# A fused attention-and-non-local kernel: VectorE's order in image 0, the seams between images and the end reordered

## The chip, the cores and the metric

The kernel runs on one core of one Trainium2 chip. The metric is the device time of one launch in microseconds (us), the median of several runs. Four images are worked through in one launch; inputs and outputs lie in HBM.

## What is computed

Two layers run one after the other on `x` of shape (4, 32, 32, 256).

```python
# layer 0: deformable attention and an MLP, per image
q      = layernorm(x) @ wq + bq
off    = conv1x1(gelu(depthwise_conv7x7_stride2(q)))       # 2 x 16 x 16 offsets
interp = grid_sample(x, refs + tanh(off))                  # 256 sampled rows
k = v  = interp @ wv + bv
attn   = softmax(heads(q @ mq) @ heads(k @ mk).T)          # 8 heads, 1024 x 256
z      = (attn @ heads(v @ mv)) @ mo + mo_b + x
y      = gelu(layernorm(z) @ mlp + mlp_b) + z
# layer 1: non-local block, per image
attn1  = softmax(theta(y) @ maxpool(phi(y)).T)             # 1024 x 256
out    = y + sigma * ((attn1 @ maxpool(g(y))) @ w_o + b_o)
```

## The kernel before, in words

Every engine has its own program, written out by hand as a list of steps; semaphores tie them together. Nothing is scheduled by a planner: an engine does its steps strictly in the order of its list, and a step that waits holds back all that stands behind it on that engine.

**Slots.** An image's attention is cut into eight units (`unit_at`: half of the rows, group of four heads, quarter of the rows). The main loop has one slot per unit, `(b, s)` with `b` the image and `s` from 0 to 7 (`slots`), and runs one slot list beyond the last image in a function `tail`. In slot `s` a unit's work is spread over three slots, so four units are in flight:

- unit `s`: `scores` in two halves (TensorE, L834, into the only score bank `ps_s`), each followed by `maxima` (VectorE, L1672), which drains that bank;
- unit `s - 1`: `max_rows` (TensorE transposes the maxima, L842), `max_out` (ScalarE, L1270), `maxima_lo` (VectorE, L1677), then two small DMAs from GpSimd's queue (`max_row`, L1982) that lay the maxima beside the queries;
- unit `s - 2`: `shifted` in two parts (TensorE, L853, into the only bank `ps_t`), each followed by `exps` (ScalarE, L1278), which drains it into `prob`;
- unit `s - 3`: `values_mixed` (TensorE, prob times values, L870) and `values_summed` (TensorE, prob times ones, L876), both into the only bank `ps_v`; then `denominators` (ScalarE, L1287 and L1289: the reciprocal as Ln and Exp) and `normalise` (VectorE, L1686), which drains `ps_v`.

`joined(b, s)` says how the two value steps lie in a slot. With None, `values_mixed` stands before the second half of the scores and `values_summed` after it, behind the second `shifted` part. With "first" both stand side by side before the second half of the scores, ScalarE makes the denominators between its two `exps`, and VectorE normalises before the second `maxima` (in slot 5 after it). With "last" both stand behind the second `shifted` part.

**Work of the neighbours.** Between these steps each slot carries dense work: the front of the next image `n` (row statistics `row_stats`, `row_scale`, `row_shift` on VectorE; `q_image`, `conv`, `offsets`, `queries`, `keys` on TensorE; `positions`, the `gather` by GpSimd's indirect DMA, `corner_weights` and `sampled`) and the back of the previous ones (`project`, `turn_rows`, `mlp_rows`, `turn_output`, `project1`, `scores1`, `max_rows1`, `shifted1`, and for the image before that `sums1`, `mix1`, `result_rows`). All dense products share a ring of three PSUM banks, in the order that `dense_order` writes out; a product waits until the one three places ahead of it has been drained.

**Image 0.** VectorE's slot 2 of image 0 has `row_stats` for image 2 (eight statistics, which wait for the loads of `xa`), ahead of the second `maxima`, and `row_scale` (eight tiles) at its end. Slots 5 and 6 have the eight steps of `sampled` for image 1, which combine the gathered corners; `corner_weights` stands in slot 4, `positions` and the gather in slot 3. In slot 6 `bias_rows` stands at the end, in slot 7 `row_shift` (half of the tiles of image 2) and `fold`.

**Seams.** In slot 7 of images 1 and 2 the non-local block of the image before takes its last maxima: `max_rows1` (L958), `max_out1` (ScalarE, L1331), `maxima1_lo` (VectorE, L1762), two small DMAs `max_row1` (GpSimd's queue, L2021), then `shifted1` (L966). SyncE's queue carries the six `stack_k` transfers of the next image at the same time. In slot 0 of image 2 VectorE has `residual_norm`, `row_shift` (the other half of the tiles, L1558), then `result` (L1786 to L1791 and L1777), which drains the banks of `mix1` (L997).

**The end.** `tail(m)` finishes image 3 and the results of image 2: `turn_rows` (L897), `norm_turned` (ScalarE, L1294), `mlp_rows` (L920), `mix1` (L997), `turn_output` (L931).

## Time and profile before

| what | value |
|---|---|
| median of 3 runs | 481.4 us (479.86 to 481.94) |
| the profiled execution's own time | 484.76 us |
| its span, first to last instruction | 482.9 us |
| mean granted TensorE clock over the span | 0.988 of full |
| TensorE busy with matmuls | 445.8 us, 92% of the span |
| VectorE, ScalarE, GpSimd busy | 60%, 43%, 23% of the span |

Times in the trace are microseconds from the start of the span. PE is TensorE's matmul stream, PEld its weight loads, DVE VectorE, ACT ScalarE, POOL GpSimd, SP SyncE. A wait is idle time of an engine just before an instruction, put down to the engine or transfer that ended last. The profiled execution lies 3.4 us above the median of the runs.

### The profile page before, as it was taken

What the parts mean: (1) busy time and instruction counts of PE and PEld (TensorE: products, weight loads), DVE (VectorE), ACT (ScalarE), POOL (GpSimd) and SP (SyncE); (2) the same over time, 40 slices, a digit from 0 to 9 for tenths busy, and PEclk for the clock granted to TensorE, in tenths of its full rate; (3) what the DMA queues carried; (4) which work ended last, traced back from release to release, by engine and by line L of the source; (5) the groups of instructions that cost most, each with busy time, mean ns of one, the idle gap of its engine ahead of it and who ended that gap; (6) DMA issues with size and microseconds to landing.
All of it is one profiled execution on the core that took longest, in us unless ns stands there. A gap on an engine that the chain in (4) does not pass through costs nothing.

```text
span 482.9 us, 9296 instructions
## 1 busy us (share of the span) xinstructions
PE 445.8 (92%) x3733; PEld 315.8 (65%) x3733; DVE 288.0 (60%) x617; ACT 209.9 (43%) x338; POOL 110.8 (23%) x150
## 2 busy tenths in 40 slices
PE   7899898797999999998999999999999998988976
PEld 6767665555668676756678666756767674655755
DVE  3719644858784277768763365476647747726343
ACT  1122113455346145765426245854273584672350
POOL 5510501041002000692002002781021030100000
PEclk9999999889999999999999999999999998999999
DMA  7498858574857960394029910494137110000112
GB/s 213 104 176 110 155 92 173 94 155 117 105 112 102 182 147 3 90 126 74 2 104 123 191 15 3 114 107 67 45 77 102 47 43 2 1 3 0 48 41 88
DMA packets 30488, 42.90 MB, mean 89 GB/s; under 512 B 6075, under 2 KB 21230, under 8 KB 30446
## 3 DMA queue, kind: packets, MB, share of 16 engines
q1 hardware_dynamic: 23742, 34.95, 39.7%
q0 software_dynamic: 3584, 4.50, 3.7%
q10 hardware_dynamic: 3120, 2.86, 3.0%
q8 instruction: 30, 0.49, 0.5%
q14 instruction: 12, 0.10, 0.1%
HBM read 16.16 MB, written 4.19 MB: 42 GB/s over the span
## 4 chain that ended last, share of the span: by engine, by line
PE 56%; DVE 16%; DMA 10%; ACT 6%; issue 5%; POOL 3%; ACTq 2%; SPq 1%; DVEq 0%; POOLq 0%
PE ps_d L785 7%; PE ps_d L920 6%; PE ps_d L887 5%; PE ps_d L997 5%; PE ps_v L870 5%; PE ps_s L834 4%; PE ps_v L876 4%; PE ps_t L853 4%; DMA xa<-in_x_dram 3%; PE ps_d L773 3%; PE ps_d L939 3%; DVE mx L1672 3%; PE ps_d L805 3%; ACTq L430 2%; DMA q_st<-mx_t 2%
## 5 line engine op out<-in xcount | busy, mean ns | idle before, releaser
L1278 ACT ACTIVATE prob<-ps_t 128x1024 f32<-128x1024 f32 x64 | 65.4, 1022 | 81.3 <-PE ps_t L853 80.2
L1672 DVE TENSOR_REDUCE mx<-ps_s 128x4 f32<-128x1024 f32 x64 | 78.2, 1222 | 19.5 <-PE ps_s L834 18.2
L1982 POOL DMA_DIRECT2D q_st<-mx_t x64 | 33.9, 531 | 235.7 <-ACT mx_t L1270 216.7
L785 PE MATMUL ps_d<-cstack,conv_w 128*32 128x256 f32 x1024 | 58.3, 380 | 0.2 <-DMA cstack<-att 0.2
L834 PE MATMUL ps_s<-k_st,q_st 96*128 96x256 f32 x256 | 49.5, 316 | 6.3 <-DVE mx L1672 4.5
L785 PEld LDWEIGHTS ps_d<-cstack,conv_w 128*32 128x32 f32 x1024 | 35.3, 108 | 21.0 <-issue 2.0
L834 PEld LDWEIGHTS ps_s<-k_st,q_st 96*128 96x128 f32 x256 | 36.3, 192 | 17.9 <-DVE mx L1672 10.9
L853 PE MATMUL ps_t<-q_st,k_st 98*128 98x256 f32 x256 | 42.8, 290 | 2.6 <-ACT zt L1336 1.0
L853 PEld LDWEIGHTS ps_t<-q_st,k_st 98*128 98x128 f32 x256 | 35.7, 193 | 5.0 <-issue 2.8
L870 PE MATMUL ps_v<-prob,vh 128*32 128x256 f32 x512 | 35.8, 398 | 2.1 <-DVE att L1686 2.1
L876 PE MATMUL ps_v<-prob,ones 128*32 128x256 f32 x512 | 35.2, 393 | 0.0
L887 PE MATMUL ps_d<-mo,att 128*128 128x256 f32 x128 | 29.7, 379 | 0.3 <-DVE att L1686 0.3
L1686 DVE TENSOR_TENSOR att<-ps_v,rden 128x256 f32<-128x256 f32 x32 | 13.4, 420 | 25.5 <-ACT rden L1289 23.0
L887 PEld LDWEIGHTS ps_d<-mo,att 128*128 128x128 f32 x128 | 23.7, 190 | 3.5 <-issue 0.5
L1677 DVE TENSOR_TENSOR mx_t<-ps_d,mx_t 4x256 fp32r<-4x256 f32 x32 | 13.3, 414 | 18.5 <-ACT mx_t L1270 17.9
L773 PE MATMUL ps_d<-wq,xln 128*128 128x256 f32 x96 | 22.4, 383 | 2.0 <-DVE xln L1558 1.7
L876 PEld LDWEIGHTS ps_v<-prob,ones 128*32 128x32 f32 x512 | 16.3, 113 | 11.3 <-issue 1.6
L2033 POOL DMA_INDIRECT corners<-in_x_dram,row_of x16 | 16.0, 999 | 33.2 <-DVE row_of L1613 29.6
L997 PE MATMUL ps_d<-gwo,zt 128*128 128x256 f32 x96 | 22.4, 384 | 0.2
L1777 DVE SCALAR_TENSOR_TENSOR z_all<-ps_d,rd,z_all 128x256 f32<-128x256 f32 x32 | 13.9, 479 | 14.3 <-PE ps_d L997 14.2
L870 PEld LDWEIGHTS ps_v<-prob,vh 128*32 128x32 f32 x512 | 14.1, 111 | 12.6 <-issue 4.4
L1270 ACT ACTIVATE mx_t<-ps_d 4x256 fp32r<-4x256 f32 x32 | 11.6, 362 | 24.6 <-PE ps_d L842 24.6
(180 smaller groups left out, 741.0 us busy)
## 6 DMA issues: line engine op xcount, KB each, us to landing
q_st<-q_parts SPq DMA_DIRECT2D x42, 256.0 KB, 5.6
xa<-in_x_dram SPq DMA_DIRECT2D x8, 512.0 KB, 8.4
z_all<-in_x_dram SPq DMA_DIRECT2D x8, 512.0 KB, 7.8
out_dram<-z_all SPq DMA_DIRECT2D x8, 512.0 KB, 2.6
cstack<-qpad SPq DMA_DIRECT2D x22, 180.5 KB, 5.7
k_st<-cstack SPq DMA_DIRECT2D x23, 128.0 KB, 3.4
q_st<-z_all SPq DMA_DIRECT2D x6, 256.0 KB, 7.0
cstack<-att SPq DMA_DIRECT2D x6, 180.5 KB, 5.3
```

The lines of the kernel that those rows point to most:

```text
L773: ins = pe.matmul(ps[:, jj, :], xln_tile(b)[:, t, cb * P:(cb + 1) * P], wq[:, kt, :], start=kt == 0, stop=kt == 1)
L785: ins = pe.matmul(ps[32 * k:32 * k + 32, 0, :], conv_w[:, cb * 4 + k, y, x, :], cstack[:, cb, k, y:y + HG_, x:x + WG_], start=n == 0, stop ...
L834: ins = pe.matmul(ps_s[:, h, :], q_st[0:96, hg * HQ + h, c0 + half * P:c0 + (half + 1) * P], k_st[0:96, b % 2, h, hg, :], start=True, stop ...
L853: ins = pe.matmul(ps_t[:, 2 * hh + mt, :], k_st[0:98, b % 2, h, hg, mt * P:(mt + 1) * P], q_st[0:98, hg * HQ + h, c0:c0 + S_], start=True, ...
L870: pe.matmul(ps_v[32 * h:32 * h + 32, 0, :], vh[:, mt, hh * HD:(hh + 1) * HD], prob[:, u % 2, h, mt, :], start=mt == 0, stop=mt == 1)
L876: ins = pe.matmul(ps_v[32 * h:32 * h + 32, 1, :], ones[:], prob[:, u % 2, h, mt, :], start=mt == 0, stop=mt == 1)
L887: ins = pe.matmul(ps[:, jj, :], att[:, hg, cb * HALF + j * P:cb * HALF + (j + 1) * P], mo[:, hg, :], start=hg == 0, stop=hg == 1)
L920: ins = pe.matmul(ps[:, jj, :], turned_tile(b)[:, kt, cb * HALF + j * P:cb * HALF + (j + 1) * P], mlp[:, kt, :], start=kt == 0, stop=kt == 1)
L997: ins = pe.matmul(ps[:, jj, :], turned_tile(b)[:, mt, cb * HALF + j * P:cb * HALF + (j + 1) * P], gwo[:, mt, :], start=mt == 0, stop=mt == 1)
L1278: drain(act.activation(prob[:, u % 2, 2 * pr:2 * pr + 2].rearrange("p h m s -> p (h m) s"), ps_t[:], ACT.Exp), t_ring, "t", b, u, pr)
L1672: drain(dve.tensor_reduce(mx[:, u % 2, half, :], ps_s[:], AX.X, ALU.max), s_ring, "s", b, u, half)
L1982: pool.dma_start(q_st[96 + part:97 + part, hg * HQ:(hg + 1) * HQ, c0:c0 + S_].bitcast(F32), mx_t[32 * part:32 * part + HQ, u % 2, :].bitca ...
```

## The change

It reorders steps and changes no arithmetic.

- Image 0: `joined` gives "first" in slots 4 to 6. On VectorE `row_stats` moves behind the second `maxima` of slot 2; `row_scale` is split, four tiles in slot 3 and four in slot 7, both behind the second `maxima`; the first half of `sampled` moves from slot 5 to the end of slot 4.
- Slot 7 of images 1 and 2: `joined` gives "last" instead of "first"; the first `project` product moves ahead of the second half of the scores.
- Slot 0 of image 2: a new value "ahead" puts both value steps and `sums1` before the first `shifted` part; VectorE's `row_shift` moves behind `result`.
- The end: the second product of `mix1(m - 1, 0)` moves ahead of `mlp_rows(m, 1)`, and its `result_rows` ahead of `outputs(m, 1, [0])`.

```diff
 def joined(b, s):
     if not b or b == B:
-        return None
-    if s == 3 or s == 6 and b < B - 1:
+        return "first" if not b and 4 <= s <= 6 else None
+    if s == 3 or s in (6, 7) and b < B - 1:
         return "last"
-    return "first" if s in (2, 4, 5, 7) or s == 1 and b < B - 1 or s == 0 and 2 <= b < B - 1 else None
+    if s == 0 and 2 <= b < B - 1:
+        return "ahead"
+    return "first" if s in (2, 4, 5, 7) or s == 1 and b < B - 1 else None
...
@@ dense_order @@
-    order += [("mlp", m, 1, jp) for jp in range(2)] + [("o", mm, 0, 1), ("o", mm, 1, 0)]
+    order += [("o", mm, 0, 1)] + [("mlp", m, 1, jp) for jp in range(2)] + [("o", mm, 1, 0)]
...
@@ TensorE, slot @@
                 if (s, b) != (0, 1):
                     scores(b, s, 0)
+                if joined(b, s) == "ahead":
+                    values(*unit_of(b, s, 3))
+                    sums1(mm)
                 if unit_of(b, s, 2):
                     shifted(*unit_of(b, s, 2), 0)
...
                 if s == 0 and fin:
-                    sums1(mm)
+                    if b >= B - 1:
+                        sums1(mm)
                     mix1(mm, 0)
...
+                if s == 7 and 0 < b < B - 1:
+                    project(b, 0, 0)
...
                     for lh in range(2):
-                        project(b, 0, lh)
+                        if lh or b == B - 1:
+                            project(b, 0, lh)
                         if post:
                             shifted1(m, lh)
...
@@ TensorE, tail @@
                 turn_rows(m, 1)
+                mix1(m - 1, 0, [1])
                 mlp_rows(m, 1)
-                mix1(m - 1, 0, [1])
...
@@ VectorE, slot @@
-                if in_front(b, s, "qimg0") and b:
+                if in_front(b, s, "qimg0") and 0 < b < 2:
                     row_shift(n, range(NJ, NT))
-                if s == 2 and b == 0:
-                    row_stats(n + 1)
...
                 if s == 0 and fin:
                     result(mm)
+                if in_front(b, s, "qimg0") and fin:
+                    row_shift(n, range(NJ, NT))
...
-                if joined(b, s) == "first" and s != 5:
+                early = joined(b, s) in ("ahead", "first") and s != 5
+                if early:
                     normalise(*unit_of(b, s, 3))
                 if cur:
                     maxima(b, s, 1)
-                if b == 0 and s in (5, 6):
-                    sampled(n, s - 5)
-                if unit_of(b, s, 3) and (joined(b, s) != "first" or s == 5) and (s, b) != (6, B - 1):
+                if (b, s) == (0, 6):
+                    sampled(n, 1)
+                if s == 2 and b == 0:
+                    row_stats(n + 1)
+                if s in (3, 7) and b == 0:
+                    row_scale(n + 1, range(NJ) if s == 3 else range(NJ, NT))
+                if unit_of(b, s, 3) and not early and (s, b) != (6, B - 1):
                     normalise(*unit_of(b, s, 3))
+                if (b, s) == (0, 4):
+                    sampled(n, 0)
...
-                if s == 2 and b == 0:
-                    row_scale(n + 1, range(NT))
...
@@ VectorE, tail @@
                 result_rows(m - 1, 0, [0])
+                result_rows(m - 1, 0, [1])
                 outputs(m, 1, [0])
-                result_rows(m - 1, 0, [1])
```

ScalarE's `denominators` and TensorE's conditions on `joined` follow the new value "ahead" as they do "first".

## Rows read from the trace of the kernel before

**Rows 1.** The page: busy time of each engine, and TensorE's clock in 40 slices

```profile
PE 445.8 (92%) x3733; PEld 315.8 (65%) x3733; DVE 288.0 (60%) x617; ACT 209.9 (43%) x338; POOL 110.8 (23%) x150
PEclk9999999889999999999999999999999998999999
```

**Rows 2.** Waits of TensorE, whole span: us in total, times, longest us

```profile
PE ps_s L834 <- DVE mx L1672: 4.5, 6, 1.2
PE ps_d L842 <- DVE mx L1672: 3.0, 4, 2.1
...
PE ps_t L966 <- DMA th_st<-mx_t: 2.4, 2, 1.4
PE ps_v L870 <- DVE att L1686: 2.1, 3, 0.8
...
PE ps_t L853 <- ACT zt L1336: 1.0, 2, 0.5
```

**Rows 3.** Timeline, image 0, slots 2 and 3: start, us, instructions, [idle before <- releaser]

```profile
86.92 1.41 DVE L1529 BATCH_NORM_STATS2 st<-xa 128x6 f32<-128x256 f32 x4 [0.39 <-DMA xa<-in_x_dram]
...
88.92 1.19 DVE L1672 TENSOR_REDUCE mx<-ps_s 128x4 f32<-128x1024 f32 x1
90.02 3.25 DVE L1547 SCALAR_TENSOR_TENSOR xa<-xa,mv,lng_all 128x256 f32<-128x256 f32 x8
...
90.25 0.38 PE L842 MATMUL ps_d<-consts,mx 128*4 128x128 f32 x2 [2.10 <-DVE mx L1672]
...
92.42 0.17 ACT L1241 ACTIVATE pos<-ps_d 128x4 f32<-128x4 f32 x1 [1.37 <-PE ps_d L797]
...
93.90 1.02 ACT L1278 ACTIVATE prob<-ps_t 128x1024 f32<-128x1024 f32 x1
...
95.03 1.23 PE L834 MATMUL ps_s<-k_st,q_st 96*128 96x256 f32 x4 [0.99 <-DVE mx L1672]
```

**Rows 4.** Windows: stretch, length, busy PE, PEld, DVE, ACT, POOL, clock, DMA share, GB/s

```profile
92.50:99.40 6.90, 5.91 (x43) 3.19 (x36) 4.61 (x12) 3.78 (x5) 2.52 (x3) 0.51 0.44 73
...
107.77:113.49 5.72, 4.49 (x52) 2.96 (x51) 3.86 (x6) 2.87 (x4) 1.04 (x2) 1.00 0.52 185
113.49:119.40 5.91, 4.55 (x54) 3.03 (x51) 4.91 (x9) 3.11 (x6) 1.04 (x2) 1.00 0.07 25
```

**Rows 5.** Timeline, image 0, slots 4 to 6, and image 1, slot 1 (146 us)

```profile
103.23 1.07 PE L876 MATMUL ps_v<-prob,ones 128*32 128x256 f32 x16
...
105.23 0.42 DVE L1686 TENSOR_TENSOR att<-ps_v,rden 128x256 f32<-128x256 f32 x1 [1.09 <-ACT rden L1289]
...
111.34 0.74 PE L834 MATMUL ps_s<-k_st,q_st 96*128 96x256 f32 x4 [1.23 <-DVE mx L1672]
...
113.64 1.53 DVE L1649 SCALAR_TENSOR_TENSOR samp<-corners,corner_w,samp 128x256 f32<-128x256 f32 x3
...
115.64 1.07 PE L870 MATMUL ps_v<-prob,vh 128*32 128x256 f32 x16 [0.82 <-DVE att L1686]
...
146.10 1.07 PE L870 MATMUL ps_v<-prob,vh 128*32 128x256 f32 x16
...
146.97 1.07 PE L876 MATMUL ps_v<-prob,ones 128*32 128x256 f32 x16
```

**Rows 6.** DMA issues with us to landing: 60:135, then 218:232, then 400:420

```profile
corners<-in_x_dram,row_of POOLq DMA_INDIRECT x4, 6.3
...
th_st<-mx_t POOLq DMA_DIRECT2D x2, 4.0 KB, 3.2
...
th_st<-mx_t POOLq DMA_DIRECT2D x2, 4.0 KB, 1.6
```

**Rows 7.** Image 2, slot 0: VectorE's timeline, and a wait of TensorE (216 to 250 us)

```profile
238.22 1.66 DVE L1558 SCALAR_TENSOR_TENSOR xln<-xa,rs,lnb_all 128x256 f32<-128x256 f32 x4
...
PE ps_d L897 <- DVE z_all L1777: 0.7, 1, 0.7
```

**Rows 8.** Waits of TensorE at the end, 440 to 460 us

```profile
PE ps_d L920 <- ACT xln L1294: 1.0, 1, 1.0
```

More of the change, by code:

```diff
@@ L1018, in slot @@
                     offsets(n)
-                if unit_of(b, s, 3) and joined(b, s) != "last" and (s, b) != (6, B - 1):
+                if unit_of(b, s, 3) and joined(b, s) not in ("ahead", "last") and (s, b) != (6, B - 1):
                     values_mixed(*unit_of(b, s, 3))
@@ L1074, in slot @@
                     values_mixed(*unit_of(b, s, 3))
-                if unit_of(b, s, 3) and joined(b, s) != "first" and (s, b) != (6, B - 1):
+                if unit_of(b, s, 3) and joined(b, s) not in ("ahead", "first") and (s, b) != (6, B - 1):
                     values_summed(*unit_of(b, s, 3))
@@ L1351, in slot @@
                     exps(*unit_of(b, s, 2), 0)
-                if joined(b, s) == "first":
+                if joined(b, s) in ("ahead", "first"):
                     denominators(*unit_of(b, s, 3))
@@ L1368, in slot @@
                     exps(*unit_of(b, s, 2), 1)
-                if unit_of(b, s, 3) and joined(b, s) != "first":
+                if unit_of(b, s, 3) and joined(b, s) not in ("ahead", "first"):
                     denominators(*unit_of(b, s, 3))
```

## The prediction, made before the changed kernel ran

> **What bounds the kernel now.** I read the page first. TensorE is busy 92% of the span and VectorE 60% [rows 1], so TensorE's stream sets the time. Only two things can shorten it: its waits, and stretches in which its clock is low. The work itself hardly changes. TensorE's waits by releaser come next [rows 2]: 4.5 us in six waits of the second half of the scores for `maxima`, 3.0 us in four waits of the transposed maxima, 2.1 us of `values_mixed` for `normalise`, 2.4 us in two waits for the small DMAs of the non-local maxima, and two waits of 0.5 us of `shifted` for the non-local exponentials. The change touches nearly all of them.
>
> The timeline then says why. In slot 2 of image 0 VectorE stands in `row_stats`, waiting for `xa` to land (86.92), so the second `maxima` comes only at 88.92 and TensorE idles 2.10 us until 90.25. Then eight tiles of `row_scale` (3.25 us) hold back the next `maxima`: 0.99 us more at 95.03 [rows 3]. Right behind these idle times the granted clock is 0.51 for 6.9 us, in which TensorE is busy 5.91 us [rows 4]; that is the lower of its two levels, 1.2 GHz against 2.4. In slots 5 and 6 TensorE works 4.49 and 4.55 us of 5.72 and 5.91 [rows 4]; there VectorE's list is too long, four sampling steps (1.53 us for three of them) in each [rows 5].
>
> **The change, part by part.**
>
> *Image 0, slots 2 to 4.* The second `maxima` no longer waits behind `row_stats`: -2.10. Four tiles of `row_scale` instead of eight, and behind the second `maxima`: -0.99 [rows 3]. `row_stats` still waits for the same landing; queued behind it is now only the next slot's `maxima_lo`, whose input comes at about the same time (88.9). In slot 4 the sums stand before the second scores and cover its 0.54 us wait, one of the six of [rows 2]. Work done at half clock takes double, so if the slow stretch does not come 5.91/2 = 2.9 us go; I take 2.7, since a part of the 5.91 lies in its edges. Against this: the second `shifted` part of slot 3 must wait for the first `exps`. That starts 1.48 us after the tanh (table load between: 92.42 to 93.90) and takes 1.02 [rows 3], so it ends 2.5 us after `offsets`, while TensorE at full clock has only the mixed values (1.07) and scores to do, about 1.6. New wait: 0.95. The values of slot 4 then wait 0.2 for `normalise`, since from the end of the sums to the end of `normalise` it is 105.65 - 104.30 = 1.35 us [rows 5]. Side by side the two value steps start 0.87 apart (146.10 and 146.97) [rows 5] instead of 1.0: -0.13. Sum: -2.10 - 0.99 - 0.54 - 2.7 + 0.95 + 0.2 - 0.13 = **-5.3**.
>
> Here a rule speaks about the clock term. The Trainium skill (TensorE: Matmul & The Clock Gate, What's actually happening) says that the throttled state is the default, that activity releases it, and that the hardware's window runs freely, so that the transition point varies from run to run. The trace agrees in that 2.10 us of idleness precede the fall; the idle times of 1.0 to 1.5 us elsewhere mostly have none behind them. By that rule the 2.7 could be absent from some runs before, and a fall could come in some runs after; both are among the rivals.
>
> *Image 0, slots 5 and 6.* They hold 9.04 us of work and 2.59 us of waits [rows 4]. The waits shown (1.23 and 0.82 [rows 5], and another 0.54) go, and merging gives -0.26. But `values_summed` used to cover the second `maxima`: now nothing stands between the second `shifted` part and the next slot's transposes, which need that `maxima`. In slot 5 `maxima` starts when the scores end, takes 1.2 us, and TensorE has only `shifted` (0.6) to do: 0.85 with the semaphores and what its delay hands on. In slot 6 `normalise` stands ahead of it and itself waits 0.93 us (105.23 - 104.30 [rows 5]) for the sums: 1.5. Slot 5's second scores wait 0.28 for `maxima`, which now stands behind `query_lo`. 2.63 of new waits: **-0.3** for both slots. Most of what is taken out of these two slots comes back as another wait.
>
> The first half of `sampled` (1.9 us) now needs its corners some 10 us earlier. Median landing is 6.3 us after issue [rows 6]; the gather starts about 4.7 us earlier than before, so I put the landing at the very moment at which slot 4 reaches it. Queued behind are `query_lo`, slot 5's `maxima`, and with them the scores. If the corners are late each us counts; bound 0 to +2, I take 0, since the same gather ran beside query stacking in the trace too.
>
> *Image 0, slot 7.* The 0.82 us wait of the values for `normalise` that remained goes (L870 waits three times in all) [rows 2], since VectorE's `sampled` no longer stands before it; `bias_rows` (1.3 us) then lies in front of the next `maxima` and costs 0.1. Four tiles of `row_scale` (1.6 us, half of 3.25 [rows 3]) fill the time in which ScalarE makes the denominators. **-0.7**.
>
> *Slot 7 of images 1 and 2.* No values stand ahead of the non-local maxima's transposes, so the small DMAs start 1.3 us earlier, and the values cover their flight. Waits now: 1.35 and 1.06 [rows 2]. With key stacking in flight they land 3.2 us (median) after issue, without it 1.6 [rows 6]. Two readings: the latency stays near 3, then 0.95 and 1.06 are gained; or the landing is tied to the end of key stacking, then 0.35 and 0.5. I take the middle: **-0.65 and -0.8**. Ends: 0 and -2.4 for the pair.
>
> A rule of the Trainium skill (DMA: Bandwidth & Descriptors, Queues, rings and completion order) bears on this: each DMA engine takes turns between its queues packet by packet. By it the earlier issue would not stand behind the key transfers, and the pair would give -2.0 rather than my -1.45.
>
> *Slot 0 of image 2.* The values and sums before the first `shifted` part cover its 0.51 us wait (L853) [rows 2]. `row_shift` (1.66 us) leaves the path to `result_rows`, which frees the bank that `turn_rows` waits 0.7 us for [rows 7]; with 0.1 beside it, -0.74. `row_shift` itself is needed by `q_image` only, 5 us later. **-1.25**. ScalarE's denominators come later, but nobody needs them soon.
>
> *The end.* `mix1` (half: 1.9 us of work that has to be done anyway) fills the 1.0 us in which `mlp_rows` waits for ScalarE [rows 8]. The bank is free and `outputs` still comes in time: **-1.0**.
>
> Sum: -5.3 - 0.3 - 0.7 - 1.45 - 1.25 - 1.0 = **-10.0 us**. The profiled execution took 484.8 us (span 482.9), so it would take about 474.8. The timed runs have a median of 481.4, 3.4 us less, and some of that may be a slow stretch that they lack. I keep the whole sum: 471.4 us.
>
> **The rivals.**
>
> *Clock.* The gain of the clock does not come, either because timed runs did not have the stretch at 92 us, or because new waits (0.95 in slot 3, 1.5 in slot 6) bring one. For: the page shows one other fall, at 398 to 411 us, after much smaller idle times, and the median is 3.4 below the profiled run. Against: 2.10 us is by far the longest idle time in the loop. Time: 481.4 - 7.3 = 474.1, with a new fall of 1.5 us 475.6. Chance 0.22.
>
> *Transfers.* The corners, and the maxima of unit 3 that GpSimd issues right behind them, come late because the gather now overlaps with query stacking; slot 5 waits up to 3 us, and the gain of slot 7 of images 1 and 2 does not come (+1.45). 481.4 - 5.5 = 475.9. For: all share 16 DMA engines. Against: 1.6 us is enough when they are free. Chance 0.12.
>
> *More gain.* The second slow stretch of the page also goes, by another phase or shift, worth about 1.6 us: 469.8. Chance 0.08.
>
> *No change.* The DVE chain of image 0 is the true bound and the next transfers take back everything, or the timed runs differ little from one another: 480.5. Against it stand the seams and the end, whose 3.7 us do not hang on image 0. Chance 0.04.
>
> *Slower.* Place: slots 3 to 7 of image 0. If the 0.95 and 1.5 us waits keep TensorE at the low level from 92 to 119 us, its 22 us of work there take 44. Some 6 us of the extra lie in waits, 2.9 were paid before: +13 against a rest of -7.3, 487. It decides where the granted clock is 0.5 for more than 14 us of image 0. For it: the fall at 92 us lasted through slot 3. Against: with waits of 1.23, 0.82 and 0.82 the clock was 1.00 in slots 5 and 6 [rows 4]. Chance 0.03.
>
> **How the numbers follow.** The forecast with its sizes as above has 0.51. Its own spread is about 3 us either way. A measurement of this kernel can tell about 0.5%, 2.4 us, from no change. Faster by more: 0.51 + 0.22 + 0.12 + 0.08 = 0.93, less 0.02 for the tail of the transfer case: 0.91. Within: 0.06. Slower: 0.03. The range goes from 468.0, where the small DMAs give their full 2.4 and the second slow stretch goes, to 477.5, where neither clock nor transfers help.
>
> **What would show it.** TensorE's 2.10 and 0.99 us waits gone, clock 1.00 from 88 to 100 us; new waits of the transposes (L842) for `maxima` at the ends of slots 5 and 6, near 0.85 and 1.5; slot 7 of image 0 reached about 5.5 us earlier and image 1 about 6.3; L966 waiting under 1 us in all; no waits of L897 for `result_rows` in image 2 or of L920 at the end. It is wrong if the clock stays low in slot 3 or 4, if `sampled` in slot 4 waits for corners, or if image 1 starts less than 4 us earlier.

## The result, and the profile after

Six runs of the changed kernel have a median of 475.94 us (475.23 to 478.65); six of the kernel before beside them 481.67. The ratio is 0.990 (95% interval 0.986 to 0.994). The time was forecast at 471.4, in a range of 468.0 to 477.5. The measured time lies inside the range, but the gain is 5.7 us by the medians and 4.9 by the ratio, about half of the 10.0 us of the sum. The profiled execution took 478.56 us, its span is 476.7.

The page: TensorE's work is the same [rows 1].

```profile
PE 444.0 (93%) x3733; PEld 316.6 (66%) x3733; DVE 288.3 (60%) x617; ACT 209.8 (44%) x338; POOL 111.2 (23%) x150
...
PEclk9999999998899999999999999999999999999999
```

The low clock at 92 us is gone, and another has come further on, in the tenth and eleventh slices. The second fall of the kernel before, in slice 34 (398 to 411 us), is absent here too; more on both below. TensorE's waits over the whole span (us in total, times, longest), beside [rows 2]; from line 130 on, line numbers are 2 to 14 higher than in the kernel before:

```profile
PE ps_d L844 <- DVE mx L1681: 3.4, 5, 1.5
...
PE ps_t L855 <- DMA q_st<-mx_t: 1.9, 3, 1.0
PE ps_s L836 <- DVE mx L1681: 1.7, 3, 0.7
...
PE ps_t L968 <- DMA th_st<-mx_t: 1.5, 2, 1.1
...
PE ps_v L872 <- issue: 0.6, 1, 0.6
```

The scores' waits for `maxima` (L836) fell from 4.5 us to 1.7. The transposes (L844) wait longer, 3.4 for 3.0, and `shifted` (L855) waits 1.9 us for small DMAs instead of 0.7. One of its three waits, 0.7 us before 86 us, is in both kernels; the two new ones, 1.14 us together, are for the DMAs of units 3 and 4 of image 0. Waits of L899 for `result_rows` and of L922 at the end no longer appear [rows 7, 8].

Where they stand, on the timeline of image 0, slots 3 (from 87.5 us) to 6 (to 117.9), against [rows 3, 5]:

```profile
92.25 0.73 PE L855 MATMUL ps_t<-q_st,k_st 98*128 98x256 f32 x4 [0.93 <-ACT prob L1287]
...
95.84 1.07 PE L872 MATMUL ps_v<-prob,vh 128*32 128x256 f32 x16 [0.59 <-issue]
...
98.29 0.65 PE L878 MATMUL ps_v<-prob,ones 128*32 128x256 f32 x4 [0.35 <-issue]
...
104.47 0.74 PE L855 MATMUL ps_t<-q_st,k_st 98*128 98x256 f32 x4 [0.17 <-DMA q_st<-mx_t]
...
109.15 0.38 PE L844 MATMUL ps_d<-consts,mx 128*4 128x128 f32 x2 [0.93 <-DVE mx L1681]
...
110.97 0.74 PE L855 MATMUL ps_t<-q_st,k_st 98*128 98x256 f32 x4 [0.97 <-DMA q_st<-mx_t]
...
117.87 0.38 PE L844 MATMUL ps_d<-consts,mx 128*4 128x128 f32 x2 [1.50 <-DVE mx L1681]
```

The three waits that the prediction gave 0.95, 0.85 and 1.5 us are there with 0.93, 0.93 and 1.50. Four others were not in the sum, or larger than in it. The wait of 0.59 has no releaser in the profile, but the program says what it is: `values_mixed` may not write `ps_v` before `normalise` has drained it. In ScalarE's and VectorE's timelines `denominators` start 0.36 us late and `normalise` ends at 95.69, 0.15 us before the values start:

```profile
94.41 0.38 ACT L1296 ACTIVATE rden<-ps_v 128x256 f32<-128x256 f32 x1 [0.36 <-PE ps_v L878]
...
95.27 0.42 DVE L1695 TENSOR_TENSOR att<-ps_v,rden 128x256 f32<-128x256 f32 x1 [1.00 <-ACT rden L1298]
```

The windows of slots 3 to 6 of image 0, each from transposes to transposes, and the two stretches of low clock (columns as in [rows 4]):

```profile
87.53:93.92 6.39, 5.46 (x63) 3.91 (x59) 6.12 (x24) 4.11 (x6) 2.31 (x4) 1.00 0.52 68
93.92:103.44 9.52, 8.58 (x63) 5.00 (x60) 6.44 (x17) 5.02 (x11) 3.80 (x5) 1.00 0.92 194
103.44:109.15 5.71, 4.61 (x51) 3.14 (x50) 4.48 (x7) 3.67 (x6) 1.04 (x2) 1.00 0.53 185
109.15:117.87 8.72, 6.24 (x51) 3.59 (x51) 3.53 (x6) 3.36 (x6) 1.04 (x2) 0.80 0.55 80
111.60:115.00 3.40, 3.40 (x33) 1.39 (x32) 0.11 (x1) 1.02 (x1) 0.00 (x0) 0.50 0.48 93
118.40:121.80 3.40, 3.40 (x24) 1.91 (x23) 3.27 (x7) 1.28 (x2) 0.84 (x2) 0.51 1.07 125
```

From 87.53 to 109.15 the clock is full. The two low stretches hold 6.8 us of work done at 1.2 GHz instead of 2.4, 3.4 us more than at full clock: as much as the one of before [rows 4] cost (2.9 us), and a little over. The first stands 0.6 us behind the wait of 0.97 and 2.5 us behind that of 0.93; the second 0.5 us behind that of 1.50. Where the falls stand differs from one profile of this same kernel to the next. In its second profile (e13) the first stands in slot 3, right behind the wait of `shifted` for `exps` that the change itself brought (0.93 us, ending at 92.6), so the low clock at 92 us is not gone for good:

```profile
92.70:96.10 3.40, 3.40 (x23) 1.82 (x24) 1.82 (x5) 1.41 (x2) 2.79 (x3) 0.50 0.51 124
116.60:120.00 3.40, 3.40 (x26) 2.16 (x24) 3.27 (x7) 1.40 (x2) 0.54 (x2) 0.50 1.08 125
```

The seams, TensorE's waits in slot 7 of image 1 and slot 0 of image 2 (212 to 250 us), then in the same stretch an image later (316 to 350):

```profile
PE ps_t L968 <- DMA th_st<-mx_t: 1.1, 1, 1.1
...
PE ps_t L968 <- DMA th_st<-mx_t: 0.4, 1, 0.4
```

On the timeline from one slot's transposes to the next, slot 7 of image 1 is 0.2 us shorter than before, slot 0 of image 2 1.6, slot 7 of image 2 0.7 and the end 1.2: 3.7 in all, forecast 3.7. So the whole shortfall lies in image 0 and in the clock.

The two profiled executions differ by 6.2 us of span (482.9 and 476.7), and image 0 has almost none of it. Its slot 3 begins 2.7 us earlier (87.53 for 90.25), slot 7 begins 1.5 us earlier, and image 1 begins (transposes of its slot 0) at 134.34 for 135.24, 0.9 us earlier, of which 0.57 were there at 72 us already, before the first step that the change moves. The prediction had called itself wrong if image 1 started less than 4 us earlier. Another 1.6 us come from the stretch between the transposes at 404 and 417 us, on which the change does not bear: there the kernel before ran 3.4 us at 1.2 GHz, and the changed kernel did not. That fall comes and goes in these kernels (the pages of six of the sixteen experiments show it), so the 1.6 us are not the change's. The window of the kernel before:

```profile
406.60:410.00 3.40, 3.40 (x32) 1.80 (x35) 2.48 (x4) 1.02 (x1) 0.52 (x1) 0.50 0.03 7
```

and of the changed kernel:

```profile
403.00:410.00 7.00, 7.00 (x63) 5.31 (x62) 5.73 (x9) 3.22 (x5) 1.56 (x3) 1.00 0.02 5
```

### The profile page after: what moved, and what is told of

Same layout as the page of the kernel before. It is cut to its first block, busy times and chain, and to the rows that moved or that the text cites. A ratio compares the mean times of both kernels' runs of the same rounds, so it can differ in the third digit from the quotient of the medians.

```text
span 476.7 us, 9296 instructions
## 1 busy us (share of the span) xinstructions
PE 444.0 (93%) x3733; PEld 316.6 (66%) x3733; DVE 288.3 (60%) x617; ACT 209.8 (44%) x338; POOL 111.2 (23%) x150
## 4 chain that ended last, share of the span: by engine, by line
PE 57%; DVE 16%; DMA 11%; ACT 6%; issue 5%; POOL 3%; SPq 1%; ACTq 0%; DVEq 0%; POOLq 0%
PE ps_d L787 9%; PE ps_d L922 6%; PE ps_d L889 5%; PE ps_d L999 5%; PE ps_v L872 5%; PE ps_t L855 4%; PE ps_s L836 4%; PE ps_v L878 4%; PE ps_d L775 3%; PE ps_d L941 3%; DMA xa<-in_x_dram 3%; DMA q_st<-mx_t 3%; PE ps_d L807 3%; DVE mx L1681 2%; DMA th_st<-mx_t 2%
## 5 line engine op out<-in xcount | busy, mean ns | idle before, releaser
L836 PE MATMUL ps_s<-k_st,q_st 96*128 96x256 f32 x256 | 49.0, 314 | 3.0 <-DVE mx L1681 1.7
L787 PEld LDWEIGHTS ps_d<-cstack,conv_w 128*32 128x32 f32 x1024 | 36.3, 108 | 19.9 <-issue 2.0
L855 PE MATMUL ps_t<-q_st,k_st 98*128 98x256 f32 x256 | 42.9, 290 | 4.2 <-DMA q_st<-mx_t 1.9
L836 PEld LDWEIGHTS ps_s<-k_st,q_st 96*128 96x128 f32 x256 | 35.8, 189 | 14.2 <-DVE mx L1681 7.2
L855 PEld LDWEIGHTS ps_t<-q_st,k_st 98*128 98x128 f32 x256 | 35.5, 192 | 7.4 <-DMA q_st<-mx_t 2.8
L807 PE MATMUL ps_d<-xln,w_qh 128*128 128x512 f32 x48 | 22.2, 594 | 0.0
L1279 ACT ACTIVATE mx_t<-ps_d 4x256 fp32r<-4x256 f32 x32 | 11.6, 363 | 23.9 <-PE ps_d L844 23.9
L922 PE MATMUL ps_d<-mlp,zt 128*128 128x256 f32 x96 | 22.0, 382 | 0.0
```

The source lines that it names most:

```text
L787: ins = pe.matmul(ps[32 * k:32 * k + 32, 0, :], conv_w[:, cb * 4 + k, y, x, :], cstack[:, cb, k, y:y + HG_, x:x + WG_], start=n == 0, stop ...
L807: ins = pe.matmul(ps[:].rearrange("p a s -> p (a s)"), w_qh[:, kt, hg * P:(hg + 1) * P], xln_tile(b)[:, kt:NT:2, half * P:(half + 1) * P], ...
L836: ins = pe.matmul(ps_s[:, h, :], q_st[0:96, hg * HQ + h, c0 + half * P:c0 + (half + 1) * P], k_st[0:96, b % 2, h, hg, :], start=True, stop ...
L855: ins = pe.matmul(ps_t[:, 2 * hh + mt, :], k_st[0:98, b % 2, h, hg, mt * P:(mt + 1) * P], q_st[0:98, hg * HQ + h, c0:c0 + S_], start=True, ...
L922: ins = pe.matmul(ps[:, jj, :], turned_tile(b)[:, kt, cb * HALF + j * P:cb * HALF + (j + 1) * P], mlp[:, kt, :], start=kt == 0, stop=kt == 1)
```

## How the runs are compared

The mean granted clock differs from run to run of one kernel, and the time with it: the 68 runs of the kernel before that stand beside the experiments give 338 us of time per unit of clock lost, all kernels of this study, each about its own mean, 337 (without the two longest of the 68 runs 325 and 331; no difference below depends on which is taken). I therefore give two numbers for each kernel: the median and ratio as measured, and **the time at full clock**, which is the mean time less 338 us times the mean clock lost. Before: 482.13 us at a mean clock of 0.9909, so 479.05 at full clock (standard error 0.1). The changed kernel, 12 runs, six of them under e13: 476.18 at 0.9942, so 474.2 (error 0.4). The change gained 4.8 us in waits and 1.1 in clock, with an error of about 0.4 on each. "At full clock" is an estimate; where it and the ratios as measured disagree, I say so.

## The experiments

```
kernel                      median  ratio to before (95%)    mean clock  at full clock
e1  image 0 only            479.40  0.995 (0.991 to 0.998)   0.9931      477.5
e2  seams and end only      476.98  0.988 (0.984 to 0.992)   0.9933      474.7
e3  image 0 apart           474.70  0.984 (0.980 to 0.988)   0.9950      473.4
e4  later z load            475.80  0.987 (0.983 to 0.991)   0.9915      472.9
e5  waits filled            475.41  0.985 (0.980 to 0.989)   0.9942      473.2
e6  statistics only         479.15  0.996 (0.993 to 1.000)   0.9942      477.8
e7  apart, gather split     474.49  0.985 (0.981 to 0.989)   0.9950      473.1
e8  gather split            475.90  0.987 (0.982 to 0.991)   0.9917      472.6
e9  sampled back            477.76  0.992 (0.989 to 0.995)   0.9912      474.8
e10 mixed                   475.92  0.988 (0.984 to 0.992)   0.9932      473.2
e11 mixed, query deferred   472.96  0.985 (0.981 to 0.990)   0.9962      472.7
e12 before, wait filled     482.18  1.001 (0.999 to 1.003)   0.9932      479.6
e13 changed kernel again    475.83  0.987 (0.983 to 0.991)   0.9940      473.7
e14 late stacking           476.50  0.989 (0.985 to 0.992)   0.9918      473.5
e15 split and back          474.38  0.985 (0.982 to 0.988)   0.9934      472.6
e16 mixed again             474.37  0.983 (0.980 to 0.986)   0.9960      472.4
```

The times at full clock have standard errors of 0.2 to 0.7. e1, e6, e9 and e12 have 12 runs each, e15 and e16 5, the others 6; each ratio is to runs of the kernel before on the same chip. Where no other base is named, an edit is against the changed kernel.

### e1 and e6: image 0's part alone, and of it only the statistics

e1 is the kernel before with all of image 0's edits (the first bullet of the change) and none of the others. e6 is the kernel before with `row_stats` and `row_scale` alone:

```diff
-                if s == 2 and b == 0:
-                    row_stats(n + 1)
...
                     sampled(n, s - 5)
+                if s == 2 and b == 0:
+                    row_stats(n + 1)
+                if s in (3, 7) and b == 0:
+                    row_scale(n + 1, range(NJ) if s == 3 else range(NJ, NT))
...
-                if s == 2 and b == 0:
-                    row_scale(n + 1, range(NT))
```

> The kernel before with only the image 0 parts of the change (side by side in slots 4 to 6, VectorE's new order). Theory: image 0 gives back what it wins, through new waits of the transposes for maxima at the ends of slots 5 and 6 (0.9 and 1.5 us), a wait of shifted for its small DMA in slot 6 (1.0 us) and granted-clock falls behind them: 0 to 2.5 us faster than before, 479 to 481.5 us. Rival: image 0 wins its 6 us in most runs and the seams fail there: 475.5 us.

> The kernel before with only row_stats and row_scale moved on VectorE in image 0. Theory: the 2.1 and 1.0 us waits of TensorE at the start of slot 3 and in it go, one 0.95 us wait of shifted for exps comes, and the clock fall behind them goes or gets shorter: -2.1 us of waits and -1 to -2.7 of clock, 478 to 479.5 us against 482. Rival, the wait moves on whole (row_stats delays maxima_lo instead): 481 us or more.

e1 gained 1.5 us at full clock where 3.6 were forecast for these parts, and 2.3 in the mean with the clock, where 6.3 were. e6 gained 1.2, and its median of 479.15 is as expected: most of what image 0 gives comes from those two steps, and `joined`, `sampled` and slot 7 add some 0.3, which is less than its error of 0.5. e1's median, 479.40, fits the theory and excludes its rival (475.5). TensorE's waits from 86 to 134 us, first e1:

```profile
PE ps_d L842 <- DVE mx L1672: 2.4, 2, 1.5
PE ps_t L853 <- DMA q_st<-mx_t: 1.6, 1, 1.6
PE ps_v L870 <- issue: 1.0, 1, 1.0
PE ps_t L853 <- ACT prob L1278: 0.9, 1, 0.9
```

and e6:

```profile
PE ps_v L870 <- DVE att L1686: 1.5, 3, 0.8
PE ps_t L853 <- DMA q_st<-mx_t: 1.4, 2, 1.3
```

In both the same wait for the small DMAs has come up, which neither `joined` nor `sampled` can have made, since e6 has neither: it is enough that slots 2 and 3 are shorter. The profiled execution of e1 was at full clock throughout image 0 in spite of waits of 1.6, 1.0 and 1.5 us, so these waits do not bring a fall every time. Its 1.0 us wait of the values is again one for `normalise`, which ends 0.15 us before them; here `denominators` started 0.81 us late.

### e2: the seams and the end alone

The changed kernel with image 0 as before (the first line of the diff, and all of VectorE's edits for `b == 0`, undone).

> The change without its image 0 parts: seams of images 1, 2 and the end only. Theory: these save what the two profiles show, 1.8 (slot 7 of image 1 and slot 0 of image 2) + 0.7 (slot 7 of image 2) + 1.2 (end) = 3.7 us: 477.9 us. Image 0 keeps its 2.1 us wait and the slow stretch. Rival (image 0 carries the gain): within 1.5 us of before, 480 us or more.

The median is 476.98 for the expected 477.9: 4.4 us at full clock, forecast 3.7, its error 0.4. These parts are right, and the rival, that image 0 carries the gain, is excluded. They are also nearly the whole of the changed kernel's 4.8: on top of them image 0 gives 0.5 (error 0.6), not 3.6.

### e3, e7 and e8: value steps apart again, and the gather in two parts

```diff
@@ e3 and e7 @@
-        return "first" if not b and 4 <= s <= 6 else None
+        return None
@@ e7 and e8: the second half of the gather a slot later @@
-                    gather(n)
+                    gather(n, range(1) if b == 0 else range(2))
+                if (b, s) == (0, 4):
+                    gather(n, range(1, 2))
```

With the gather cut, only two of its four DMAs stand in GpSimd's queue ahead of unit 3's small DMAs; those are issued at 96.28 us in e8, where the changed kernel has 97.23, and two gather DMAs fewer are in flight with them. They land 6.3 us after issue in e8 and 5.1 in e7, so part of what the cut gives is the earlier issue.

> The changed kernel with the value steps of image 0 apart again, as before; VectorE's new order stays. Theory: the sums again cover maxima at the ends of slots 5 and 6, the waits of 0.9 and 1.5 us go, no clock fall follows: 2 to 4 us faster than the changed kernel, 472 to 474 us. Rival: values_mixed waits 0.8 us for normalise in each slot as in the kernel before and takes it back: 475.5 to 476.5 us.

> The changed kernel with the value steps of image 0 apart and the gather cut in two. Theory: the two repairs are independent, but with the steps apart slot 5 is bound by VectorE's list, not by the small DMAs: 474 to 474.7 us, no slower than with the steps apart alone (474.7). Rival, the effects add: 473.5 us or less.

> The changed kernel with image 0's gather cut in two: its first half in slot 3, its second behind the small DMAs of unit 3. Theory, transfers: these DMAs no longer stand in GpSimd's queue behind four gathers, the wait of shifted in slot 5 (0.2, 1.1 and 1.7 us in three profiles) and any wait of sampled for corners go: slot 5 near 5.5 us, 0.5 to 1.5 us less than the changed kernel, 474.5 to 475.5 us. Rival, the query stacking alone makes them late: the same waits and time.

None of the three medians settles its expectation cleanly: e3 has 474.70, between theory (472 to 474) and rival (475.5 to 476.5), e7 474.49 inside its theory, e8 475.90 just above its (474.5 to 475.5). Apart, with or without the cut, the kernel is faster by 0.8 to 1.1 us at full clock; the medians of the 12 runs of e3 and e7 together and of the 12 of the changed kernel are 474.5 and 475.9. Resampling these runs gives a ratio of the means of 0.9975 (0.995 to 1.000), from several chips, so this is at the limit of what can be told. So with the gather whole, side by side did not help. With the gather cut (e8 and e7) the two ways are 472.6 and 473.1 at full clock, not to be told apart. The lengths of the slots, each from transposes to transposes, say what side by side does where no transfer is late and no fall lies in the slot:

```
us                  slot 3  slot 4  slot 5  slot 6  slot 7   from
side by side          6.39    7.93    5.71    5.82   14.95   e4; slot 5 of e14
apart                 6.39    8.86    5.71    5.33   15.84   e6; slots 5 to 7 of e7
```

It gains 0.9 in slot 4, nothing in slot 5, loses 0.5 in slot 6, and gives 0.9 in slot 7, since no value wait is left there. The waits of the transposes eat what slots 5 and 6 gain, as forecast; what side by side costs beside that is the cover of the small DMAs, and clock. The 47 runs with it in slots 5 and 6 and these waits left open (changed kernel, e4, e8, e9, e14, e15) have a mean clock of 0.9924 (error 0.0005), the 29 with the steps apart there (e3, e7, e10, e11, e16) 0.9950 (0.0007): 0.9 us. e7's waits, 86 to 134 us:

```profile
PE ps_s L836 <- DVE mx L1681: 2.3, 3, 1.2
PE ps_v L872 <- DVE att L1695: 1.1, 2, 0.8
```

No wait for DMAs is left (nor has e3 one, with the gather whole, in a profile in which a fall made slot 3 1.3 us longer). In e8 none is left either, but VectorE then stood waiting for the corners, and the scores behind it for 1.2 us. VectorE's timeline of e8 in slots 4 and 5:

```profile
102.26 0.35 DVE L1655 TENSOR_SCALAR samp<-corners,corner_w 128x256 f32<-128x256 f32 x1 [1.51 <-DMA corners<-in_x_dram,row_of]
...
104.09 1.41 DVE L1595 SCALAR_TENSOR_TENSOR q_parts<-ps_d,cols,q_parts 128x512 fp32r<-128x512 f32 x2
...
105.97 1.22 DVE L1681 TENSOR_REDUCE mx<-ps_s 128x4 f32<-128x1024 f32 x1
```

`query_lo`, slot 5's lower maxima and its `maxima` queue behind the late corners, as the transfer rival has it. At full clock e8 is still 1.6 us under the changed kernel (error 0.7); its median is the same, since its runs had a lower clock (0.9917).

### e4 and e14: which transfer makes the small DMAs late

```diff
@@ e4, SyncE: the z load a slot later @@
                     if s == 3:
                         behind_max_row(b, 3)
+                    if s == 4:
+                        behind_max_row(b, 4)
                         load_z(b)
@@ e14, SyncE: a query stacking a slot later @@
-                    if s == 2:
-                        behind_max_row(b, 2)
-                        stack_q(b, 1, [1])
                     if s == 3:
                         behind_max_row(b, 3)
+                        stack_q(b, 1, [1])
                         load_z(b)
```

> The changed kernel with image 0's z load issued one unit later, behind the small DMAs of unit 4. Theory: the 1.0 us wait of shifted in slot 6 for these DMAs (behind 1 MB of z load) never occurs; with it one of the two idle times that stood before the first clock fall is gone: 0.5 to 1.5 us less than the changed kernel, 474.5 to 475.5 us. Rival, the wait is seldom there in the timed runs: same within 0.5 us.

> The changed kernel with the stacking of image 0's second query half (one part of it) issued a slot later, behind unit 3's step and ahead of the z load. Theory A, the stacking takes the DMA engines from the gather and the small DMAs: the wait of the first shifted part of unit 3 (1.1 to 1.9 us in most profiles) falls under 0.3, and the corners are there when sampled comes. Theory B, the small DMAs are late because GpSimd's queue has the gather ahead of them: the wait stays at 1.1 to 1.9 us. In either case the first scores that read the half moved may wait, up to 1 us, in slot 6; the median then stays within 0.3% of the changed kernel's.

In e4 (median 475.80, expected 474.5 to 475.5) the wait in slot 6 (110.97 above) is absent, and that in slot 5 is 2.8 us: the z load has no part in the lateness of unit 3's DMAs. That it makes unit 4's late fits, but is not shown: e5, e8, e9 and e15 leave it where it was, and do not have the wait either. For unit 3's DMAs e14 decides. The DMA issues of 95 to 100 us, with us to landing, in e4:

```profile
q_st<-mx_t POOLq DMA_DIRECT2D x2, 4.0 KB, 7.4
```

The same of 94 to 99 us in the changed kernel:

```profile
q0 software_dynamic: 158, 0.52, 50.5%
q1 hardware_dynamic: 256, 0.49, 48.1%
...
q_st<-mx_t POOLq DMA_DIRECT2D x2, 4.0 KB, 6.4
```

and in e14:

```profile
q0 software_dynamic: 287, 0.95, 65.7%
...
q_st<-mx_t POOLq DMA_DIRECT2D x2, 4.0 KB, 2.8
```

q1 is query stacking, q0 the gather with the small DMAs. Together they fill the 16 engines (98.6% in the changed kernel), and 4 KB take 6.4 us to land. In e14 the same four gather DMAs stand ahead of the small ones in GpSimd's queue, stacking is out of the way, and they land in 2.8. The wait of `shifted` for them is gone, and VectorE does not wait for the corners either (0.9 us in e13). So it is query stacking on the shared engines, as theory A has it, not the order of GpSimd's queue. The median did not fall (476.50): the scores of slot 6 now wait 0.7 us for the queries moved and 0.4 more for `maxima`, a fall of the clock begins there (108.5 us), and the mean clock was lower (0.9918). e14's waits, 86 to 134 us:

```profile
PE ps_d L842 <- DVE mx L1679: 2.1, 2, 1.1
...
PE ps_s L834 <- DMA q_st<-z_all: 0.7, 1, 0.7
...
PE ps_s L834 <- DVE mx L1679: 0.4, 1, 0.4
```

### e9 and e15: the first half of `sampled` back in slot 5

```diff
@@ e9 and e15 @@
-                if (b, s) == (0, 6):
-                    sampled(n, 1)
+                if b == 0 and s in (5, 6):
+                    sampled(n, s - 5)
...
-                if (b, s) == (0, 4):
-                    sampled(n, 0)
@@ e15 alone: the gather cut as in e7 @@
```

> The changed kernel with the first half of sampled back in slot 5, steps still side by side. Theory: sampled never waits for its corners (1.5 us in two profiles), but slots 5 and 6 are bound by VectorE's list again and every maxima comes later: 0 to 1.5 us slower than the changed kernel, 476 to 477.5. Rival, the wait for corners is what slot 5 pays: 1 us faster, 475 us or less.

> The changed kernel with the gather cut in two (second half a slot later) and the first half of sampled back in slot 5. No work is left out. Theory of the transfers: no wait of shifted for unit 3's small DMAs and none of sampled for corners; what is left are the waits for maxima, and because VectorE has four sampling steps more in slot 5, slots 5 and 6 together lose 1 to 2 us to maxima. The median is then between the changed kernel's and 0.5% above. Rival, that the DMA waits cost the whole of what is missing: 0.4 to 0.6% below the changed kernel.

e9 takes the early need of the corners away and keeps everything else. Its median of 477.76 is at the upper end of its theory (476 to 477.5) and excludes the rival. It came out at 474.8 at full clock, no better than the changed kernel (474.2): the small DMAs alone cost it 1.9 us in its profile. e15 has neither DMA wait and reaches 472.6; its median of 474.38 lies below its theory (no faster than the changed kernel) and just short of the rival's 0.4 to 0.6% below it. e9 and e15 differ in nothing but the cut, and this is the clearest figure for the lateness of the small DMAs: 2.2 us at full clock (error 0.4), or 1.7 (0.5) if each is taken against the kernel before on its own chip. That corners needed early are worth having once the small DMAs are in time is not shown: e8, which has them early, is at 472.6 as well.

### e5 and e12: do small waits bring the low clock?

Products whose results nobody reads, put on TensorE ahead of the transposes; no wait is taken away.

```diff
@@ e5, changed kernel; e12, kernel before: 4 products if (b, u) == (0, 2) @@
                 ps = open_bank(dense, "mxt", b, u)
+                for _ in range({5: 2, 6: 3}.get(u, 0) if b == 0 else 0):
+                    pe.matmul(ps[:, 1, :], ident, w_kh[:, 0, :], start=True, stop=True)
```

> The changed kernel with two and three dummy 128x256 products (0.43 us each, into the unused half of the transposes' bank) in the two new waits of TensorE at the ends of slots 5 and 6 of image 0. No work is taken away and the waits themselves stay; if they cause the clock falls, the granted clock stays 1.00 through slots 5 to 7: 1 to 2 us less than the changed kernel in the median (474 to 475 us), and no run near 478.5. Rival, the falls have another cause: same time and the same falls, or 0.2 us more.

> The kernel before with four dummy 128x256 products (1.73 us) inside TensorE's 2.1 us wait at the start of image 0's slot 3. The wait and all other work stay. Theory: if the wait brings the clock fall at 92 us, that fall goes; worth up to 2.7 us where it stood, 1 to 2 us in the median since some runs lack it: 480 to 481 us, mean granted clock up by about 0.004. Rival, the tiny products of offsets cause it as well: no difference.

e12 is the experiment on the clock term, with 480 to 481 us expected. It fills the 2.10 us wait that precedes the fall of [rows 4] and leaves the time as it is: 482.18 against 482.06 (ratio 1.001, 0.999 to 1.003). Its windows behind the next wait, that of the scores for `maxima`, 1.74 us at 92.6 to 94.3:

```profile
92.70:94.80 2.10, 0.51 (x4) 0.51 (x5) 1.97 (x6) 1.39 (x2) 0.50 (x1) 1.00 0.02 4
94.80:98.20 3.40, 3.40 (x25) 1.82 (x25) 1.65 (x5) 1.37 (x2) 1.76 (x2) 0.51 0.70 117
```

The work that the first wait had delayed now waited at the second, and the fall came 2 us later behind that one; in this profile it lasted 3.4 us where the kernel before had 6.9. The runs have a mean clock of 0.9932 (error 0.001) for 0.9909, worth 0.8 us, and 0.5 more at full clock takes that back. So filling that wait alone did not give the 2.7 us; a gain of some tenths in clock cannot be excluded. In e5 the profile is free of a fall in slots 4 to 7 and no run is over 477.0, but the median (475.41) misses the 474 to 475 expected, and the mean clock is the changed kernel's, 0.9942: the profile agrees with the theory that filling helps, the six runs do not show it. At full clock e5 is 1.0 us under the changed kernel (error 0.7) though no wait was taken away; differences of this size from six runs can be chance.

### e10, e11, e13 and e16: a better order

```diff
@@ e10, e11 and e16, beside the gather cut of e7 @@
-        return "first" if not b and 4 <= s <= 6 else None
+        return "first" if not b and s == 4 else None
...
-                if (b, s) == (0, 6):
-                    sampled(n, 1)
...
                 if (b, s) == (0, 4):
                     sampled(n, 0)
+                if (b, s) == (0, 6):
+                    sampled(n, 1)
@@ e11 and e16: the second part of query_lo behind slot 5's first maxima @@
+                if (b, s) == (0, 5):
+                    query_lo(n, 0, [1])
...
-                    query_lo(n, 0)
+                    query_lo(n, 0, range(NHG) if b else [0])
```

> The changed kernel with the steps side by side only in slot 4, apart in slots 5 and 6, normalise ahead of the second half of sampled in slot 6, and the gather cut in two. Theory: slot 4 near 7.9 us as side by side, slot 5 near 5.7, slot 6 near 5.3 and the 0.8 us wait of the values in slot 7 gone: 1.5 us less than with the steps apart everywhere, 473 us. Rival, corners come late and VectorE takes it back: 474.5 us.

> As e10_mixed, and the second query_lo of image 1 stands behind slot 5's first maxima instead of before slot 5's maxima_lo. Theory: the 1.2 us wait of the second scores in slot 5 for maxima shrinks by 0.6: 472.5 us. Rival, that wait has moved elsewhere already: same as e10_mixed.

> The changed kernel once more, unaltered, as the control of the three others. If the ratio measured for it holds, 0.990 (0.986 to 0.994) against the kernel before. Theory of the transfers: its profile has at least one of the two waits in slots 4 and 5 of image 0, of the transposes or of shifted for unit 3's small DMAs (0.2 to 1.9 us) or of sampled for the corners. Rival, that those waits were a matter of one profile: none of them.

> The best version once more (side by side only in slot 4, normalise ahead of sampled in slot 6, the gather cut in two, one part of query_lo later), beside the changed kernel on the same chip. If its gain is real: 0.984 to 0.987 against before, and 0.3 to 0.6% under the changed kernel. If its first measurement was luck of the clock: within 0.2% of it.

Side by side in slot 4 only, `normalise` ahead of `sampled` in slot 6, the gather cut: 473.2 at full clock for e10, whose median (475.92) misses the 473 expected. With `query_lo` in two it is 472.7 and, run again, 472.4; what `query_lo` adds is inside the errors. The 11 runs of e11 and e16 have a median of 473.1; against the 12 of the changed kernel the ratio of the means is 0.9952 (0.992 to 0.998, resampled), some 2.3 us. Beside each other on one chip, e16 and e13: 0.983 (0.980 to 0.986) and 0.987 (0.983 to 0.991) of the kernel before. e16 lies 0.4% under e13 in the mean, as expected of a real gain. This version beats both kernels. At full clock it is level with e8 and e15 (472.6); its lead over them as measured, 473.1 for 475.3, goes with the clock (0.9961 for 0.9925). Its profiled execution (e11) took 472.84 us, at full clock in all 40 slices; its waits, 86 to 134 us:

```profile
PE ps_s L836 <- DVE mx L1681: 1.8, 2, 1.1
PE ps_t L855 <- ACT prob L1287: 0.9, 1, 0.9
PE ps_t L855 <- DMA q_st<-mx_t: 0.6, 1, 0.6
PE ps_v L872 <- DVE att L1695: 0.5, 2, 0.2
```

3.8 us in these four lines, where the four of e1 have 5.9. VectorE still waited 1.4 us for the corners in it, and 1.8 in e16. e13's own profile has 0.47 and 0.62 us of `shifted` waiting for small DMAs and 0.9 of `sampled` for the corners, so those waits of the changed kernel were no matter of one profile.

## Why the prediction was right or wrong

**Slots 2 and 3, the order of VectorE.** Right. The 2.10 and 0.99 us waits are gone and 0.93 has come for 0.95; slot 3 takes 6.39 us from transposes to transposes. In e6 these two edits are 1.2 us at full clock, of the 2.1 that the sum has for them; 1.3 us wait there for the small DMAs. One reading was off without effect: the 0.54 us wait of slot 4's second scores is not one of the six for `maxima`, the profile gives it no releaser.

**Slots 5 and 6.** The new waits of the transposes are right to 0.1 us (0.93 for 0.85, 1.50 for 1.5), and so is the reading that side by side gives back what it takes. The terms shown add up to -0.2, not -0.3.

**Image 0 as a whole.** Where nothing is late the forecast for it holds. Slot 2 is 2.1 us shorter, slots 3 and 4 take 14.3 us for 17.5, slots 5 and 6 11.5 for 11.6, slot 7 14.95 for 15.84 (the table under e3): 6.3 us in all, the sum's own figure (-5.3 - 0.3 - 0.7), put together from undisturbed slots of several profiles. In the changed kernel's profile slots 4 to 7 lost 1.6, 0, 2.9 and 1.5 us of it again: 3.4 by the two falls, 1.0 by the small DMAs of unit 4, 1.6 in slot 4.

**The transfers. This is the step that failed,** a term put at nothing: "the landing at the very moment at which slot 4 reaches it", "bound 0 to +2, I take 0, since the same gather ran beside query stacking in the trace too". The prediction looked at the corners; what came late first was what GpSimd issues behind them. Before, unit 3's small DMAs were issued at 101.71, 6.1 us behind the first of the stacking transfers (95.59), and landed after 5.2. In the changed kernel they are issued at 97.23, 3.4 us behind it (93.79), while stacking and gather hold 98.6% of the engines, and land after 6.4, which is later than `shifted` wants them. That cost 0.2, 1.6, 1.3, 1.1, 2.8, 1.9 and 0.5 us in seven profiles with the gather whole (changed kernel, e1, e6, e5, e4, e9, e13), and nothing in an eighth (e3). Unit 4's small DMAs, issued behind the z load, cost 1.0 and 0.6 us in the changed kernel's two profiles; VectorE waits 0.9 to 1.8 us for the corners where they are late (e13, e8, e5, e11, e16). That is the rival of transfers, to which I gave 0.12 and the time 475.9. That the measured 475.94 meets this time is luck, for it is not that rival alone: the gain of slot 7 of images 1 and 2, which it gives up, came in part, 0.2 and 0.7 us of 0.65 and 0.8. At full clock removing the small DMAs' lateness gave 1.6 us (e8, e15; errors 0.5 to 0.7), of the 2.5 that are missing in waits, and 2.2 (0.4) from e9 to e15.

**The values of slot 4** waited 0.59 us for `normalise`, where 0.2 were forecast; in e4, e6, e8, e9 and e11 it is 0.24, as forecast. What is late is ScalarE's first step of `denominators`, by 0.36 us here. Then `values_summed` and ScalarE's `exps` stood still without a releaser in the profile: from the start of the values to the end of the sums it is 3.10 us where e4 has 1.93. Slot 4 took 9.52 us where e4 has 7.93.

**The clock: mis-sized.** 2.7 us were counted; the mean granted clock rose from 0.9909 to 0.9942, which is 1.1. The 2.10 us wait did not by itself set the loss (e12): in these profiles falls stand behind waits of 0.93 (e13), 0.97, 1.50, 1.74 and 2.10 us, and not in each run. The new waits in slots 5 and 6 had falls behind them in the profiled execution, and the runs that have them are 0.9 us poorer in clock than those with the steps apart. The clock rival had this with 0.22 and 474.1 to 475.6. The Trainium skill (TensorE: Matmul & The Clock Gate, What's actually happening) has the throttled state as the default and the point of transition as varying from run to run; the runs agree: in the 68 of the kernel before the mean clock goes from 0.981 to 1.000. A term worked out from one profiled execution should have been weighed by that.

**Seams and end.** Right: 3.7 us on the timeline for 3.7, 4.4 (error 0.4) in e2. The shares differ, so that the total is right is in part luck: slot 7 of image 1 gave 0.2 for 0.65, since `th_st` still lands in 3.9 us beside key stacking; slot 7 of image 2 0.7 for 0.8; slot 0 of image 2 gave 1.6 for 1.25, the end 1.2 for 1.0. `th_st` waits 1.5 us in all, where the prediction looked for less than 1, and the 2.0 us that the pair would give if the issue did not stand behind the key transfers did not come.

**The sum.** Forecast 10.0 us: 7.3 of waits, 2.7 of clock. Found 4.8 and 1.1 over all runs. The missing 4.1 are 2.5 of waits, of which the small DMAs are shown to be some 1.6, and 1.6 of clock. What stays open is the rest of the waits, and with it why ScalarE and the sums of slot 4 stand still in some executions.

## What to carry to other kernels

When slots are shortened, every transfer that is issued inside them meets its neighbours at another time: for each small DMA on the path, take what fills the engines at its new time of issue, and add the difference in landing as a term. Price a clock term at its mean over runs, not at what one profiled execution shows, and count the new waits against it. An edit that takes a wait from one step and hands it to the next gains nothing by itself (slots 5 and 6: 11.53 us side by side, 11.63 before), and the waits that it makes can bring falls of the clock.

## What the hardware showed that was not expected

- Two 4 KB DMAs of GpSimd's queue took 2.8 us to land with the gather alone on the engines (e14). With query stacking beside the gather they took 5.0 to 5.2 where they were issued about 6 us behind the start of stacking (e2, kernel before), 5.7 to 7.4 where it was 3.1 to 5.4 us (changed kernel, e1, e3, e4, e5, e6, e9, e13; the sooner behind stacking, the later they landed, almost in order), and 4.9 to 6.6 with the gather cut in two (e7, e8, e10, e11, e15, e16).
- Filling a wait of TensorE with work moved the clock's fall to the next wait (from 92.5 in the kernel before to 94.8 us in e12) without a gain in time.
- From 95.8 to 98.3 us of the changed kernel three engines stood still for a time with no releaser that the profile shows: ScalarE 2.57 us, VectorE 0.58, TensorE 0.35. ScalarE's line of the timeline:

```profile
98.34 1.03 ACT L1287 ACTIVATE prob<-ps_t 128x1024 f32<-128x1024 f32 x1 [2.57 <-remote]
```

At the same place the values start 0.36 to 1.25 us late in e1, e5 and e14, each time 0.15 us behind `normalise`, and ScalarE had begun `denominators` 0.1 to 1.0 us late; in the others the values start 0.3 us late at most. Its cause was not tried.
